# Dividing two attentions by their sums: 32 reciprocals per partition, gathered by token and spread back with the unit matrix

## The reference

```python
# favor attention (first layer)
num = jnp.einsum('bhmd,bhm->bhd', kv, q)
den = jnp.einsum('bhm,bhm->bh', q, ksum)
attn = num / den[..., None]
main = attn @ out_w + out_b
...
# softmax attention (second layer)
att = jnp.einsum('bhqd,bhkd->bhqk', q, k) / jnp.sqrt(jnp.float32(HD))
att = jax.nn.softmax(att, axis=-1)
out = jnp.einsum('bhqk,bhkd->bhqd', att, v)
```

## Time and profile before

| | |
|---|---|
| time, median of 3 runs | 2227.73 us (2225.33 to 2232.55) |
| time of the profiled execution | 2232.31 us |
| its span, first to last instruction | 2230.5 us |
| granted TensorE clock, mean | 0.941 of full |
| busy: PE, PEld, DVE, ACT, POOL | 1846.4, 1070.3, 1322.2, 776.0, 272.5 us |
| share of the chain that ended last: PE, DVE, ACT | 50%, 28%, 8% |

### The profile page before, as it was taken

How to read it: one execution, slowest core, us unless ns; L and a number is a source line. 1 busy time by engine, 2 the same in 40 slices (tenths; PEclk the granted TensorE clock), 3 DMA queues, 4 the chain that set the end, 5 groups by cost and what they waited for, 6 DMA issues and landing times.

```text
span 2230.5 us, 43273 instructions
## 1 busy us (share of the span) xinstructions
PE 1846.4 (83%) x18116; PEld 1070.3 (48%) x18116; DVE 1322.2 (59%) x2712; ACT 776.0 (35%) x1441; POOL 272.5 (12%) x222
## 2 busy tenths in 40 slices
PE   1788898888888888888988879788898888988877
PEld 1355444554454544545445455354444554444644
DVE  1566457675476654766547655656556665476644
ACT  0322343323432335223352333522443324523234
POOL 0101102101011011010210101101111101021010
PEclk9999899999998999989999999999999999999889
DMA  4000200002000020000200011000200002000020
GB/s 174 1 6 2 29 2 11 1 2 29 2 11 1 2 29 7 6 1 6 25 7 7 2 16 15 6 6 2 27 5 6 6 2 29 2 6 1 2 29 7
DMA packets 27476, 29.77 MB, mean 13 GB/s; under 512 B 3524, under 2 KB 25844, under 8 KB 26740
## 3 DMA queue, kind: packets, MB, share of 16 engines
q1 hardware_dynamic: 27284, 27.01, 6.3%
HBM read 12.06 MB, written 2.36 MB: 6 GB/s over the span
## 4 chain that ended last, share of the span: by engine, by line
PE 50%; DVE 28%; ACT 8%; SPq 6%; issue 4%; DMA 4%; POOL 0%; ACTq 0%; DVEq 0%
SPq L430 5%; PE bank L726 5%; PE bank L948 4%; DMA phi<-parts 4%; PE bank L938 3%; PE bank L758 3%; PE bank L923 3%; DVE ls L1444 2%; DVE ftm L1370 2%; DVE parts L1380 2%; PE bank L1037 2%; DVE lmx L1432 2%; PE bank L961 2%; DVE lc L1426 2%; PE bank L664 2%
## 5 line engine op out<-in xcount | busy, mean ns | idle before, releaser
L1605 DVE TENSOR_REDUCE amx<-bank 128x2 f32<-128x512 f32 x256 | 163.0, 685 | 69.5 <-PE bank L961 69.5
L1593 DVE TENSOR_TENSOR mh<-bank,silu 128x512 f32<-128x512 f32 x144 | 98.8, 691 | 149.8 <-PE bank L938 112.3
L1209 ACT ACTIVATE silu<-bank 128x512 f32<-128x512 f32 x144 | 84.2, 597 | 268.8 <-PE bank L923 256.7
L948 PEld LDWEIGHTS bank<-w_mw,mh 128*128 128x128 f32 x1152 | 144.8, 201 | 27.1 <-issue 27.1
L923 PE MATMUL bank<-xn2T,w_mw 128*128 128x512 f32 x288 | 153.1, 657 | 0.0
L948 PE MATMUL bank<-w_mw,mh 128*128 128x128 f32 x1152 | 151.7, 287 | 0.0
L1624 DVE RECIPROCAL ftm<-bank 128x512 f32<-128x512 f32 x16 | 53.7, 3357 | 165.2 <-PE bank L1044 165.2
L664 PE MATMUL bank<-hT,w_wqkv 128*128 128x512 f32 x256 | 119.0, 602 | 17.2 <-ACT hT L1069 11.0
L1432 DVE TENSOR_REDUCE lmx<-bank 128x4 f32<-128x512 f32 x128 | 79.5, 684 | 87.3 <-PE bank L726 87.3
L1444 DVE RECIPROCAL ls<-bank 128x256 f32<-128x256 f32 x64 | 112.1, 1751 | 23.8 <-PE bank L778 23.8
L466 POOL TENSOR_TENSOR lc<-lc,ls 128x512 f32<-128x512 f32 x32 | 41.0, 1280 | 679.7 <-DVE lc L1402 679.7
(11 more groups left out here) (283 smaller groups left out, 3682.4 us busy)
## 6 DMA issues: line engine op xcount, KB each, us to landing
phi<-parts SPq DMA_DIRECT2D x96, 64.0 KB
lc<-parts SPq DMA_DIRECT2D x96, 64.0 KB
w_mw<-in_mw SPq DMA_DIRECT2D x3, 1152.0 KB
x_in<-in_x SPq DMA_DIRECT2D x8, 256.0 KB, 2.7
out<-res SPq DMA_DIRECT2D x8, 256.0 KB, 2.3
w_wqkv<-in_wqkv SPq DMA_DIRECT2D x1, 1536.0 KB
w_w<-in_w SPq DMA_DIRECT2D x1, 682.0 KB
mh<-in_rotary SPq DMA_DIRECT2D x1, 512.0 KB
```

Of the source, the lines that this page charges most:

```text
L948: last = mm(bank_of("final")[:, t], mh[:, (2 * q + i) % 4, t], W["mw2"][:, ORDER[q], i, :], start=(q == 0 and j == 0 and i == 0), stop=Fal ...
L1209: A(silu[:, n % 2, :], bank_of("moe_g", n)[:], ACT.Silu).then_inc(sem["moe_silu"], 1)
L1593: V.tensor_tensor(mh[:, n % 4, :], bank_of("moe_u", n)[:], silu[:, n % 2, :], ALU.mult).then_inc(sem["moe_h"], 1)
L1605: V.tensor_reduce(amx[:, 2 * b:2 * b + 2, h], bank_of("att_max", n)[:].rearrange("p (t k) -> p t k", t=2), AX.X, ALU.max).then_inc(sem["at ...
```

## The change

Each denominator's matmul with `den` is turned round: the heads are now the stationary operand and `den` is a 128 x 8 selector, four small products, one for each block of 128 columns. The result has tokens on the partitions and 4 x 8 = 32 denominators in each. DVE takes 32 reciprocals per partition into `quot`, copies each 16 times next to itself into `ftm` (128 x 512), and PE multiplies the four blocks of `ftm` by the unit matrix (`spread_quotients`), which turns them back to features by tokens in the same PSUM bank. DVE then multiplies `heads` by that bank instead of by `ftm`. The operations on both engines are placed in these lists:

```diff
@@ constants
-    den = np.zeros((P, P))
-    den[p // 16 * 16 + 8, p] = 1
+    den = np.zeros((P, 8))
+    den[np.arange(8) * 16 + 8, np.arange(8)] = 1
@@ PE
                 def favor_den(b):
                     pe.wait_ge(sem["favor_sums"], now("favor_sums", b + 1))
-                    mm(bank_of("favor_pv", b)[:], W["den"][:], heads[:, b, :], start=True, stop=True).then_inc(
-                        sem["favor_den"], 1)
+                    for i in range(4):
+                        last = mm(bank_of("favor_pv", b)[:, 8 * i:8 * i + 8], heads[:, b, i * P:(i + 1) * P], W["den"][:],
+                                  start=True, stop=True)
+                    last.then_inc(sem["favor_den"], 1)
+
+                def spread_quotients(o):
+                    for i in range(4):
+                        last = mm(o[:, i * P:(i + 1) * P], ftm[:, i, :], I[:],
+                                  start=True, stop=True)
+                    return last
+
+                def favor_rows(b):
+                    pe.wait_ge(sem["favor_rec"], now("favor_rec", b + 1))
+                    spread_quotients(bank_of("favor_pv", b)).then_inc(sem["favor_rows_ps"], 1)
...
                         if n == 0:
                             favor_den(l)
+                        if n == 1:
+                            favor_rows(l)
...
+                def att_rows(b):
+                    pe.wait_ge(sem["att_rec"], now("att_rec", b + 1))
+                    spread_quotients(bank_of("att_pv", b)).then_inc(sem["att_rows_ps"], 1)
...
                     if pair == 12:
                         att_den(0)
+                    if pair == 14:
+                        att_rows(0)
                 att_project(it, 0)
                 att_den(1)
                 if it + 1 < TURNS:
                     favor_values(it + 1)
-                else:
+                att_rows(1)
+                if it + 1 == TURNS:
                     att_project(it, 1)
@@ DVE
-                def favor_out(b):
-
-                    share = ftm[:].rearrange("p t d -> p (t d)")
-                    dve.wait_ge(sem["favor_den"], now("favor_den", b + 1))
-                    link(V.reciprocal(share, bank_of("favor_pv", b)[:]))
-                    V.tensor_tensor(heads[:, b, :], heads[:, b, :], share, ALU.mult).then_inc(sem["favor_att"], 1)
+                def quotients(s, o):
+                    link(V.reciprocal(quot[:, s, :], o[:, 0:32]))
+                    return V.tensor_copy(ftm[:].rearrange("p t (h r) -> p (t h) r", r=16),
+                                         quot[:, s, :].unsqueeze(2).broadcast_to([P, 32, 16]))
+
+                def favor_quotients(b):
+                    dve.wait_ge(sem["favor_den"], now("favor_den", b + 1))
+                    quotients(0, bank_of("favor_pv", b)).then_inc(sem["favor_rec"], 1)
+
+                def favor_out(b):
+                    dve.wait_ge(sem["favor_rows_ps"], now("favor_rows_ps", b + 1))
+                    V.tensor_tensor(heads[:, b, :], heads[:, b, :], bank_of("favor_pv", b)[:], ALU.mult).then_inc(
+                        sem["favor_att"], 1)
...
-                    favor_out(l)
+                    favor_quotients(l)
                     for n in range(4):
...
+                        if n == 0:
+                            favor_out(l)
...
                 for b in range(G):
-                    share = ftm[:].rearrange("p t d -> p (t d)")
                     dve.wait_ge(sem["att_den"], now("att_den", b + 1))
-                    if b:
-                        dve.wait_ge(sem["att_o"], now("att_o", 1))
-                    V.reciprocal(share, bank_of("att_pv", b)[:]).then_inc(sem["att_rec"], 1)
-                    dve.wait_ge(sem["att_rec"], now("att_rec", b + 1))
-                    V.tensor_tensor(heads[:, b, :], heads[:, b, :], share, ALU.mult).then_inc(sem["att_o"], 1)
+                    quotients(1, bank_of("att_pv", b)).then_inc(sem["att_rec"], 1)
+                    dve.wait_ge(sem["att_rows_ps"], now("att_rows_ps", b + 1))
+                    V.tensor_tensor(heads[:, b, :], heads[:, b, :], bank_of("att_pv", b)[:], ALU.mult).then_inc(sem["att_o"], 1)
```

More of the change, by code:

```diff
@@ L37 @@
     "xnT_ps": 1, "favor_qk_ps": 2, "favor_map_ps": 8, "favor_v_ps": 1, "favor_score_ps": 32,
-    "favor_pv": 8, "favor_den": 2, "favor_out_ps": 1,
+    "favor_pv": 8, "favor_den": 2, "favor_rows_ps": 2, "att_rows_ps": 2, "favor_out_ps": 1,
     "loc_raw_ps": 16, "loc_ss_ps": 4, "loc_sum_ps": 2, "loc_rT_ps": 2, "loc_rb_ps": 8, "loc_v_ps": 8,
@@ L51 @@
     "route_T": 1, "moe_w": 8,
-    "xn": 1, "favor_v": 1, "favor_p": 32, "favor_att": 2, "favor_res": 1,
+    "xn": 1, "favor_v": 1, "favor_p": 32, "favor_att": 2, "favor_rec": 2, "favor_res": 1,
     "loc_c": 16, "loc_sum": 2, "loc_rs": 2, "loc_qk": 16, "loc_mx": 16, "loc_nm": 4,
@@ L160, in build @@
         warm = sb("warm", [P, 1])
+        quot = sb("quot", [P, 2, 32])
         x_in = sb("x_in", [P, TT, D])
@@ L1043, in att_den @@
                     pe.wait_ge(sem["att_sums"], now("att_sums", b + 1))
-                    mm(bank_of("att_pv", b)[:], W["den"][:], heads[:, b, :], start=True, stop=True).then_inc(
-                        sem["att_den"], 1)
+                    for i in range(4):
+                        last = mm(bank_of("att_pv", b)[:, 8 * i:8 * i + 8], heads[:, b, i * P:(i + 1) * P], W["den"][:],
+                                  start=True, stop=True)
+                    last.then_inc(sem["att_den"], 1)
+                def att_rows(b):
+                    pe.wait_ge(sem["att_rec"], now("att_rec", b + 1))
+                    spread_quotients(bank_of("att_pv", b)).then_inc(sem["att_rows_ps"], 1)
                 for pair in range(G * AH // 2 + 2):
```

## The result

| | before | changed |
|---|---|---|
| time, median of 4 runs each | 2227.71 us | 2270.65 us (2266.39 to 2276.1) |
| ratio, 95% interval | | 1.0191 (1.0163 to 1.0219) |
| profiled execution: time, span | 2232.31, 2230.5 us | 2271.31, 2269.5 us |
| granted clock, mean | 0.941 | 0.944 |
| busy PE, PEld, DVE | 1846.4, 1070.3, 1322.2 us | 1884.6, 1119.4, 1240.8 us |

What follows compares the result with a forecast made beforehand. In the local attention PE was taken as the bound from L738 on. On the profiled execution, 2232.3 + 44.8 - 2.8 - 1.1 = 2273.2 us; as a median about 2227.7 + 40.9, or 2269 us, range 2258 to 2284.

Steps and rivals of the forecast that it cites:

- The cause: Local attention: the favor product frees its bank later, so L738 starts 2.80 us later, 16 times, 44.8 us lost; chance 0.81.
- the spreading: Favor attention on PE, between scores of part 1 and sums of part 0: four fp32 products, 0.89 us, bounds 0.85 to 1.2.
- The other links: Favor chain: sums to local reciprocal 0.82 us, reciprocal and gap 1.79, local to favor product 0.61, favor product to L738 0.75.
- The `den` products: Favor attention on PE: four small fp32 products cost 0, bounds a gain of 0.2 us and a loss of 0.2.
- The copy: DVE's 128 x 512 copy within SBUF after the short reciprocal: 0.6 us, bounds 0.54 and 0.69.
- The turn's end: Softmax attention, sequence 1: `favor_map(0)` (L581) comes 0.4 us earlier, 7 times, 2.8 us gained; bounds 0 and 1.0 each.
- the last turn: End of the softmax attention, where nothing lies between the product and the projection: 1.1 us gained.
- `att_rows(0)`: Softmax attention, sequence 0, 0.89 us between scores of pairs 14 and 15: costs 0, bounds 0 and 0.9 a turn.
- PE bounds the stage: Local attention: PE is the bound from L738 on, so DVE being ready earlier there gives PE nothing back.
- the rival: DVE bounds the local attention: 2.4 us saved a layer, 38 us in all, time 2186; chance 0.05.
- The clock: Rival: the clock falls in the new waits, PE then at half rate; 2293 to 2301 if every time; chance 0.08.
- The price per fall: Local attention behind the new wait: each fall of the clock costs 1.5 to 2 us.

Runs made afterwards that it cites:

- the bank swap: Changed kernel with transposes of the second row maxima given the other of banks 6 and 7, not the one favor's numerators lie in: 2232.45 us, ratio 1.0018.
- the order put back: Changed kernel with the favor product moved on DVE directly behind the quotients, ahead of the first local reciprocal: 2230.88 us, ratio 1.0008.
- the short reciprocal: Kernel before, with the favor reciprocal over the first 32 of 512 columns only and nothing added on PE: 2220.73 us, ratio 0.9964.
- its own experiment: Softmax attention as changed, favor attention as in the kernel before: 2231.0 us, ratio 1.0013.
- the early denominators: Changed kernel with den products ahead of the first maxima's transposes, spreading behind the first scores, favor product right behind its quotients: 2222.8 us, ratio 0.9972.
- the one with GpSimd held back: Early denominators, softmax spreading of sequence 0 moved from pair 14 to 16, and GpSimd's product waiting for layer 0's quotients: 2211.84 us, ratio 0.9926.

## Why the prediction was right, point by point

**The cause.** Right, and shown by the bank swap and by the order put back. PE waits 2.12 us for the heads product, 16 times, 33.9 us in all (2.1, 16, 34 predicted). From the first transposes to those of the second four heads in the second turn's second layer it was 7.62 (L738 at 464.97 and 472.59); now it is 10.61 (L751 at 469.24 and 479.85). That is 2.99 later, 2.80 predicted.

**The term that was mis-sized** is the spreading. Taken from L560 as 0.89, it measures 392.37 - 391.28 = 1.09, though shape and count are the same; the next line's first weight load follows eight fp32 records 0.2 later here. This is within the bounds of 0.85 to 1.2, and it is all of the difference. At the turn's end the same eight records take 614.90 - 614.02 = 0.88, so the place matters; why is not shown. The other links held: sums to reciprocal 393.19 - 392.37 = 0.82, as predicted; 1.79 to the local product; 0.61 to the favor product; 0.73 to L751 (0.75). That the product now reads PSUM costs nothing (0.68). The `den` products, put at 0, cost 0: from the first transposes to the 32 products of part 1 it is 388.51 - 384.39 = 4.12 before and 389.83 - 385.71 = 4.12 now.

**The copy** was put at 0.6 with a lower bound of 0.54 and took 0.427. The bound was wrong: it took 342 ns for 128 columns and 0.5 ns for each of 384 more. From 342 to 427 ns it is only 0.22 ns a column, an estimate across two different operations. The estimate of about 0.4 by the Trainium skill ("VectorE: DVE Perf Modes", the perf-mode tier table) was the better one, and the trace agrees with it at 0.427. In the changed kernel nobody waits for it, so the sum did not suffer. The 32-column reciprocal took 0.358 (0.35).

**The turn's end.** From the load of the `den` products to `favor_map(0)` it was 5.40 and is 616.83 - 612.04 = 4.79: 0.61 gained, 0.4 predicted, the quicker copy and the wait gone. In the last turn, from the same load to the start of the projection, it was 2225.08 - 2219.78 = 5.30 and is 2264.87 - 2260.96 = 3.91: 1.39 gained (1.1), and 0.8 more behind it, since the projection itself took 1.16 instead of 1.95 after a wait of 0.8 instead of 4.2. `att_rows(0)`, put at 0, costs 0.28 to 0.54 a turn, 3.6 us in all: the two exponentials in stock did not cover the spreading wholly. That leaves 4.3 + 2.2 - 3.6 = 2.9 us gained in the trace, where I had 3.9; its own experiment shows no gain in time.

**PE bounds the stage.** Right: the short reciprocal gave 8 us, not the 38 of the rival.

**The clock.** I named a clock below 1.00 behind the wait as a sign that I was wrong, and it was below behind 5 of 16: 0.53 to 0.56 four times, 0.71 once. The price per fall was about right, 1.61 four times and 1.31 once, where 1.5 to 2 was given. The step that failed was the argument from the earlier trace rows: that a wait of 2.13 kept the clock in the three places I had read does not say that the next one will. The trace of the kernel before even held the counter-example, in the last of its eight waits of this length, which I had not read (the row of the timeline, then the window of 3.4 us that starts with it):

```profile
2078.21 0.40 PE L738 MATMUL bank<-w_ident,lnm 128*128 128x128 bf16 x4 [2.13 <-DVE lmx L1432]
```

```profile
2078.21:2081.61 3.40, 3.40 (x36) 2.66 (x40) 0.97 (x3) 1.88 (x2) 0.00 (x0) 0.54 0.00 0
```

**The total** came nearer than its terms, and that is in part luck. With the measured ones it is 16 x 2.99 = 47.8, less 7 x 0.61 = 4.3 for the turn ends and 2.2 for the last, plus 3.6 for sequence 0: 44.9, where mine was 40.9. The five falls add 7.8, which makes 52.7. The medians differ by 42.9 and the two spans by 39.0. So some 14 us came back in the profiled execution, in stretches with the same instructions in both kernels (feed-forward part, router and experts), at a higher granted clock where I compared them (0.92 against 0.89). My sum had neither the falls nor this, and the two largely cancelled. What sets the clock in those stretches no run settles.

**DVE** lost 81.4 us of busy time (77 predicted; the copy's 0.17 x 32 is the difference), and of that the time saw nothing.

## What to carry to other kernels

A shorter instruction on an engine that is waited for by nobody buys only the last wait at its place, here 0.28 us of 3.0. When a step is split in two, look at what the second half releases: here the product that frees a PSUM bank slipped behind a reciprocal and a product of another chain, and the wait for the bank cost more than everything saved. And work that is added to the bound engine belongs into one of its waits: moving the denominators under the wait for the maxima, the spreading under the wait for the exponentials, and GpSimd's product out of the copy's way turned +1.9% into -0.7%.

## What the hardware showed that I had not expected

A copy of 128 x 512 fp32 within SBUF takes 427 ns alone and 1371 ns beside GpSimd's product of 1.26 us, in the first layer of a turn, while the reciprocal from PSUM just ahead of it overlaps the start of the same product and takes its usual 0.35 us. The view of that one line in the kernel with the early denominators (min/median/max in ns), and in the one with GpSimd held back:

```profile
L1391 DVE COPY ftm<-quot x32: 426/427/1371, 114.8 to 2216.2; 128x512 f32<-128x512 f32 x32
```

```profile
L1392 DVE COPY ftm<-quot x32: 426/427/428, 117.7 to 2202.8; 128x512 f32<-128x512 f32 x32
```

The copy's read and write both lie in SBUF. The Trainium skill ("SBUF — State Buffer", SBUF: two separate sides) has DVE, in its quick copy mode within SBUF, and GpSimd share a port pair, and whoever starts first keeps it for a whole instruction. The trace agrees in the order of events: GpSimd's product starts first, at 382.39, and ends at 383.65; the copy, issued at 382.57, ends at 383.94. That is 0.29 behind the product, less than the 0.43 which the copy takes alone, so the trace does not show that it stood still to the product's very end (the ends of GpSimd's spans are rough). That the lock is the mechanism is argued from this; that GpSimd's product is the cause is shown by holding it back.

And the clock: the length of a wait did not tell whether it falls. Waits of 2.12 us were followed by a clock of 0.53 to 0.71 in 5 places of one kernel and of 1.00 in 11 places of the same kernel; waits of 2.13 us in the kernel before, by 0.54 in one place and 1.00 in seven. And stretches with the same instructions ran at 0.89 in one turn and at 0.92 in another, which is worth 1.4 us of 64, without a change in the program that explains it.
